# Expert stage of a decoder layer: two transfers behind each single-tile pass wait for the next up weights

## The reference, cut to what matters

```python
h = _rms(x, w_ln2).reshape(B * S, H)             # 2048 rows of 512
logits = h @ w_router
probs = jax.nn.softmax(logits, axis=-1)
top_w, top_i = jax.lax.top_k(probs, TOP_K)       # 2 of 8 experts a row
combine = jnp.sum(jax.nn.one_hot(top_i, N_EXP, dtype=h.dtype) * top_w[..., None], axis=1)
g = jnp.einsum('th,ehi->eti', h, w_gate_e)       # 512 -> 352
u = jnp.einsum('th,ehi->eti', h, w_up_e)
y = jnp.einsum('eti,eih->eth', jax.nn.silu(g) * u, w_down_e)   # 352 -> 512
routed = jnp.einsum('eth,te->th', y, combine)
sh = jax.nn.silu(h @ w_sh_gate) * (h @ w_sh_up) @ w_sh_down
sh = sh * jax.nn.sigmoid(h @ w_sh_eg)
x = x + (routed + sh).reshape(B, S, H)
```

## Time and profile before

| | us |
|---|---|
| median of 3 runs | 2419.51 |
| lowest and highest | 2418.83, 2424.62 |
| the profiled execution | 2418.0 |
| its span, first to last instruction | 2416.3 |
| granted TensorE clock over the span, share of full speed | 0.997 |
| PE busy in the span | 2331.6 |
| DVE, ACT, POOL busy | 1348.2, 1341.1, 917.4 |
| the routed part, from the first single's pass on (1976.5 to 2202) | 225.5 |

### The profile page before, as it was taken

How to read it: one execution, slowest core, us unless ns; L and a number is a source line. 1 busy time by engine, 2 the same in 40 slices (tenths; PEclk the granted TensorE clock), 3 DMA queues, 4 the chain that set the end, 5 groups by cost and what they waited for, 6 DMA issues and landing times. The chain is left out here.

```text
span 2416.3 us, 38332 instructions
## 1 busy us (share of the span) xinstructions
PE 2331.6 (96%) x15092; PEld 1495.5 (62%) x15092; DVE 1348.2 (56%) x2103; ACT 1341.1 (56%) x1696; POOL 917.4 (38%) x610
## 2 busy tenths in 40 slices
PE   9999999999999999999999999999899999999998
PEld 8887444444454444444334556665678898998886
DVE  6677544434444434434423656556675577777785
ACT  4333677667766777767896434433422256665222
POOL 2228755565455445555302343432024122221320
PEclk9999999999999999999999999999999999999999
DMA  6004833546344643455542300001045367776431
GB/s 227 18 18 128 293 119 127 186 142 201 121 164 129 219 149 112 155 180 182 171 139 83 123 2 1 19 10 64 36 134 180 101 210 253 256 248 204 147 110 47
DMA packets 203649, 326.67 MB, mean 135 GB/s; under 512 B 69168, under 2 KB 123696, under 8 KB 203312
## 3 DMA queue, kind: packets, MB, share of 16 engines
q1 hardware_dynamic: 184112, 246.50, 30.7%
q0 software_dynamic: 16336, 72.23, 9.0%
q10 hardware_dynamic: 3024, 5.51, 0.7%
HBM read 238.39 MB, written 96.27 MB: 139 GB/s over the span
## 5 line engine op out<-in xcount | busy, mean ns | idle before, releaser
L1115 ACT ACTIVATE A_c_prob<-c_psum 128x1024 f32<-128x1024 f32 x832 | 786.9, 1029 | 273.7 <-PE c_psum L1380 271.2
L1040 POOL TENSOR_TENSOR E_c_roots<-E_c_roots,c_half 128x32 f32<-128x32 f32 (+1 forms) x70 | 361.4, 5165 | 401.7 <-DVE E_c_roots L1132 401.6
L1391 PE MATMUL c_psum<-A_c_prob,c_vq 128*17 128x512 f32 x3328 | 413.0, 596 | 8.6 <-DVE c_oT L1278 8.4
L143 PE MATMUL c_psum<-E_c_w,E_c_c 128*128 128x512 f32 x1248 | 311.9, 399 | 1.4 <-DVEq L1260 0.7
L143 PEld LDWEIGHTS c_psum<-E_c_w,E_c_c 128*128 128x128 f32 x1248 | 226.7, 188 | 122.0 <-issue 41.5
L1380 PE MATMUL c_psum<-c_qq,c_kq 64*128 64x512 f32 x1664 | 285.5, 435 | 12.5 <-ACT A_c_prob L1115 9.7
L1380 PEld LDWEIGHTS c_psum<-c_qq,c_kq 64*128 64x128 f32 x1664 | 135.6, 184 | 155.6 <-ACT A_c_prob L1115 84.1
L1172 DVE COPY E_c_unit<-c_psum 128x256 f32<-128x256 f32 x89 | 37.8, 425 | 328.5 <-PE c_psum L143 328.5
L2785 PE MATMUL m_psum<-A_m_dn_hi,A_m_a 128*128 128x512 f32 (+1 forms) x576 | 187.8, 394 | 4.2 <-DVE A_m_a L2523 4.2
L1391 PEld LDWEIGHTS c_psum<-A_c_prob,c_vq 128*17 128x17 f32 x3328 | 68.5, 96 | 187.6 <-issue 163.8
L143 PE MATMUL m_psum<-R_g_hi,U_s_up 128*128 128x512 f32 x528 | 170.0, 395 | 0.6 <-DVEq L2504 0.6
(11 more groups left out here) (361 smaller groups left out, 3948.9 us busy)
## 6 DMA issues: line engine op xcount, KB each, us to landing
c_kq<-kd SPq DMA_DIRECT2D x120, 416.0 KB, 5.7
kd<-S_c_t SPq DMA_DIRECT2D x96, 256.0 KB, 2.7
E_c_raw<-in_ctxT SPq DMA_DIRECT2D x89, 256.0 KB, 3.5
qd<-A_c_q SPq DMA_DIRECT2D x32, 512.0 KB, 4.1
c_qq<-qd SPq DMA_DIRECT2D x64, 256.0 KB, 3.1
vd<-A_c_vt SPq DMA_DIRECT2D x104, 136.0 KB, 1.8
c_vq<-vd SPq DMA_DIRECT2D x30, 442.0 KB, 4.9
S_up_raw<-in_sup SPq DMA_DIRECT2D x20, 512.0 KB, 6.5
```

What stands on the lines that cost most here:

```text
L143: mm = pe.matmul(out, a(c), b(c), start=first and i == 0, stop=last and i == len(terms) - 1)
L1040: pool.tensor_tensor(rr[:, unit % RB, 0:n], ms[:, unit % RB, 0:n], half[:, 0:n], ALU.pow).then_inc(s_r, 1)
L1115: act.activation(prob[:, t % PB, 2 * (u % 2):2 * (u % 2) + 2, :], score_banks[u % 3], ACT.Exp, scale=XD ** -0.5).then_inc(s_ex, 1)
L1391: mm = pe.matmul(o_bank[32 * j:32 * j + VW, :], vq[:, q % 2, kt, j, :], prob[:, t % PB, j, :], start=kt == 0, stop=kt == CT - 1)
```

## The change

Two waits are added in `moe`, and nothing else. Both are on `s_up_picked[1]`, the count of landed up gathers of j = 1.

```diff
             def load_rows(tile):
+                if 3 <= tile < NTILES and passes[R0 + tile - 3].turned:
+                    sp.wait_ge(s_up_picked[1], 16 * tile)
                 if tile == 0:
                     sp.wait_ge(s_gu, 2 * base(R0 - 1))
...
             def pick_down(tile):
                 pool.wait_ge(s_dnlo, UNITS + tile)
+                if tile and tile + 1 < NTILES and passes[R0 + tile - 1].turned:
+                    pool.wait_ge(s_up_picked[1], 16 * (tile + 2))
                 if tile == 0:
```

## The result

| | before | after |
|---|---|---|
| median of 5 runs each, us | 2423.02 | 2441.81 |
| lowest and highest | 2418.83, 2424.62 | 2435.98, 2443.69 |
| the profiled execution | 2418.0 | 2443.69 |
| its span | 2416.3 | 2442.0 |
| the stretch 1976.5 to 2202: PE busy of 225.5 | 218.19 | 207.08 |

The account below looks back on a forecast made before the run. PE, busy 96% of the span, was taken to bound the kernel. Five places (+0.26, +1.32, +1.33, +0.71, +1.50) summed to +5.1 us, taking the median of 2419.51 to 2424.6 us; range 2416.0 to 2431.0.

Parts of the forecast that it names:

- the clock behind PE's stops: After PE's stops behind singles: no term for a clock fall; each stop priced at its own length.
- D: Behind each single, time from the j = 1 gather's issue to the down weights' landing: 12.17 us, 11.77 behind tile 19.
- the ceiling: Routed part behind the first single: PE's stops, 7.31 us in all, are the most the change can gain.
- Part one: Behind each single, with the rows load held: the j = 1 up gather lands in 5.7 us; holding rows costs nothing.
- my sum: Over the five places behind singles: PE's added loss from later down weights, together +5.1 us.
- Part two, the issue at 0.27 us behind the landing: On POOL, the held down gather goes out 0.27 us after the j = 1 gather's landing.
- Part two, the down gather at 6.2 us: Held down gather, meeting the rows load and the result's store: takes 6.2 us, 5.8 behind tile 19.
- The 0.3 us for the next up gather: Within the down gather's time: 0.3 us added for the head of the up gather queued behind it.
- The new wait takes the old one's place: Behind each single: ACT waits for down weights; PE stops 2.2 to 2.6 us ahead of the down product, not chunk 0.
- The second rival, the meeting transfers: At the five held down gathers: transfers share the engines, gather takes 7.0 us, sum +11.1 us, 2430.6; chance 0.17.
- The order of the two gathers: On POOL's ring: in-order rule says holding the down gather gives j = 1 nothing; sum would be 1.5 us less.
- the losing side: Whole kernel: the outcome of measuring slower rather than about the same, counted from D = 12.6 us on; chance 0.24.

Follow-up runs that it names:

- experiment 1: Against the changed kernel: the down gather's wait removed, only the rows load's wait kept; 2413.33 us, ratio 0.9964 to the kernel before.
- experiment 2: Against the changed kernel: the rows load's wait removed, only the down gather's wait kept; 2439.43 us, ratio 1.0067 to the kernel before.
- experiment 6: Against the changed kernel: the rows load waits for the down gather's landing instead, down gather's wait kept; 2429.88 us, ratio 1.0027 to the kernel before.
- experiment 4: Against the changed kernel: the next up gathers also wait until the down gather has landed; 2444.16 us, ratio 1.0087 to the kernel before.
- experiment 7: Against the changed kernel: only the store of the single's result also waits for the down gather's landing; 2444.05 us, ratio 1.0087 to the kernel before.
- experiment 3: Against the changed kernel: PE runs filler transposes while it waits ahead of five down products; 2433.52 us, ratio 1.0044 to the kernel before.

## Why the prediction was wrong, point by point

Two steps failed. The prediction put the clock behind PE's stops at nothing (11.4 us in the profile after), and it sized D too short: 6.2 us for the down gather where 7.0 were measured, and 0.27 us for POOL's issue where it was 0.74 to 1.05 (together with the j = 1 gather 7.7 us). On the median that the prediction stood on, either alone would have put the time beyond the range (2436 and 2432 against 2431).

- **What bounds the kernel, and the ceiling.** Right. PE's 7.3 us of stops are the whole gain to be had, and experiment 1 took nearly all of them (7.6 us in the medians; in the profile the distances between the t0 shrank by 7.1).
- **Part one, the j = 1 gather at 5.7 us.** Right: 6.20, 5.45, 5.53, 6.26 and 5.57, 0.5 us in all over my sum. Holding the rows costs PE nothing through their own landing, also right; what they cost the down gather comes below.
- **Part two, the issue at 0.27 us behind the landing.** Mis-sized. The landings are at 1993.66 (ACT and SP start there), POOL's issue at 1994.40: 0.74 us, and the five places add up to 4.0 against my 1.35. The 0.27 is POOL's reaction to DVE; no row of before showed it behind a landing. That is 2.7 us.
- **Part two, the down gather at 6.2 us.** The term that I called deciding was the most mis-sized of D. It took 7.8, 6.7, 7.5 and 7.2 us beside a rows load of 0.52 MB (5.8 beside the one of 0.26 MB): 4.5 us in all. The 5.8 was predicted, with luck: 0.26 MB less at 403 GB/s takes 0.65 us off 6.2, not 0.4, so my own working gives 5.55. The meeting with SP's transfers is the mechanism that I gave; experiments 2 and 6 show it, 5.4 us on average where the rows had gone out 9 us earlier, 4.9 where rows and store were behind it. My sum moved the bytes at 403 GB/s. Windows of the changed kernel while the first of these gathers is under way show that rate only at the end, and less than half of it at first, though the DMA engines are busy 0.68 of the time:

```profile
1996.00:1998.00 2.00, 2.00 (x19) 2.00 (x19) 2.00 (x5) 1.26 (x4) 1.70 (x2) 1.00 0.68 199
1998.00:2000.00 2.00, 2.00 (x19) 2.00 (x18) 1.02 (x3) 0.00 (x0) 0.75 (x1) 1.00 0.85 318
2000.00:2002.00 2.00, 2.00 (x19) 2.00 (x19) 0.00 (x0) 0.00 (x0) 0.00 (x0) 1.00 1.07 417
```

  I had taken the rate from a stretch in which all transfers were already running. These rates count every transfer, the next up gathers too, so they show that 403 GB/s was wrong for the start but not what held the gather back. The 0.3 us for the next up gather was wrong: experiment 4 has nothing for it.
- **The new wait takes the old one's place.** Right in each step: ACT's wait at the down split, five times, and PE's single stop ahead of the down product. The second rival, the meeting transfers at +11.1 us, is what the landings did; they came to 12.8. I had put 0.17 on it. Its mechanism is right for the rows load and the store and wrong for the next up gather (experiment 4), and what separates +12.8 from the measured time is the clock, which it didn't have either.
- **The clock.** The step that failed outright, and more than half of the miss: 11.4 of the 19.0 us by which the profile missed the sum, 8 to 10 of 13.7 in the medians. The prediction priced a stop of PE at its own length. It wrote down stops of 2.2 to 2.6 us in one piece, and no case of it had a fall of the clock behind them. Experiment 6, with stops of 1.83 to 2.66 us, lost 6.4 us to the clock, so even stops as short as predicted weren't free. The trace of before gave no row on it, since its stops, 1.61 us and after 3 us of work 0.69, left the clock at 1.00. That was a reason to bound the cost, as for every other thing the trace didn't show, and the range should have had it.
- **The order of the two gathers.** By the rule that I cited from the Trainium skill ("DMA: Bandwidth & Descriptors", section on queues, rings and completion order) the second wait gives the first gather nothing and the next up gather takes nothing from the down gather. Experiments 2 and 4 agree with it. I wrote that it would take 1.5 us off the sum, and kept them in. A wait that can't gain should be priced as pure loss. The sum did so, but the chance of the losing side, 0.24, did not.

What the terms make together: 5.1 us predicted, + 0.5 (j = 1) + 2.7 (POOL) + 4.5 (down gather) = 12.8, + 11.4 (clock) = 24.1 of the profiled execution. The medians differ by less, 18.8 us, mostly because the profiled execution of before was 5.0 us faster than its median.

## What to carry to other kernels

Holding back a transfer helps a more urgent one only if the two really compete. The load on the other queue did (the first j = 1 gather went from 8.1 to 6.2 us); the gather behind it on the same queue did not, and it was itself urgent by the time it was let go. Two transfers released by one semaphore start together, here 0.75 to 1.05 us apart: what is held back for a landing meets everything else that waits for it. And when a change moves several short stops of PE into one longer one, add the clock behind it to the price.

## What the runs showed of the hardware

- Around PE stops of 2.4 to 5.5 us the granted clock was at 0.50 for 3 to 7 us, in part still within the stop; in the profile after that cost 1.5 to 2.6 us a time, over all runs 1.3 to 2.85. Length alone doesn't decide: stops of 2.37 (experiment 6), 3.05 and 3.10 (experiment 2) and 3.42 us (experiment 7) left it at 1.00, and stops of 1.81 (experiment 7), 1.83 and 1.90 us (experiment 6) were followed by 0.50. Which stops bring a fall, no run here settles. Stops of 1.61 and 0.69 us with 3 us of work between left it at 1.00.
- POOL issued a gather 0.74 to 1.06 us behind the landing that it waited for (by ACT's start on the landed half), SP a load 0.0 us behind it (1993.65 against 1993.66).
- A gather of 0.79 MB took 5.0 us with nothing beside it (issued at 1950.96 in the kernel before), and 4.7 to 5.4 in experiment 6, with further gathers queued behind it and nothing of SP beside it. Beside a load of 0.52 MB that started 0.75 to 1.05 us before it, and a store of 0.26 MB behind that, it took 6.2 to 8.1 us (the changed kernel twice, and experiments 3 and 4); with the load alone beside it 6.0 to 7.2 (experiment 7).
- All transfers together moved 199 GB/s in the changed kernel from 1996 to 1998, while such a gather was under way, and 417 GB/s from 2000 to 2002.
